# Edge stage of a graph network layer: the second layer's message stays in PSUM, and the first half of the pipeline moves by one slot

## What is computed

```python
x = concatenate((h[i], h[j], w), axis=-1)
msg = silu(x @ mW1 + mb1)
msg = layer_norm(msg, ln_g, ln_b)
msg = silu(msg @ mW2 + mb2)
agg = segment_sum(msg, i, num_segments=3125)
```

## The kernel before

| step | engine, line | slot |
|---|---|---|
| gather of 2 x 128 rows of `b_table` into `g_rows` | GpSimd, L961 | p |
| one-hot `ohT` of the target, from `loc_rows` (loaded by SyncE) | VectorE, L1164 | p+1 |
| first matmul, row of `a_sb` into `psH` | TensorE, L1057 | p+2 |
| `g_rows` += `psH` ("hid") | VectorE, L1178 | p+2 |
| silu 1 into `act1` | ScalarE, L1006 | p+4 |
| statistics (two `bn_stats`) | VectorE, L1184 | p+4 |
| variance (five small steps), each three pairs | VectorE, L1130 to L1142 | at j = 1, 4 |
| power -1/2 of the variance ("root"), each three pairs | GpSimd, L950 | at j = 0, 3 |
| shift, each three pairs | VectorE, L1150 | at j = 0, 3 |
| normalisation into `normed` (two) | ScalarE, L992 | p+10 |
| four transposes into `psM` | TensorE, L1077 | p+11 |
| copy to `nT` | ScalarE, L1002 | p+12 |
| second layer into `ps2` (four fp32 matmuls, eight passes) | TensorE, L1085 | p+13 |
| silu 2 from `ps2` to `msg` | ScalarE, L985 | p+15 |
| `high` = `msg` rounded to fp32r | ScalarE, L998 | p+15 |
| one-hot `ohf` of the target | VectorE, L1169 | p+15 |
| `low` = `msg` - `high` | VectorE, L1190 | p+15 |
| sum of high and low parts by target into `psG` | TensorE, L1067, L1068 | p+17 |
| `agg` += `psG` | VectorE, L1117 | p+18 |

## Time and profile before

### The profile page before, as it was taken

The page is one execution under the profiler, slowest core; times in us unless marked ns, Lnnn a source line. Parts: engine busy times, 40 slices in busy tenths (PEclk is TensorE's granted clock), DMA queues, the critical chain, the costliest instruction groups (busy, mean ns, idle before and its releaser), DMA issues. The chain is left out here.

```text
span 2091.9 us, 47075 instructions
## 1 busy us (share of the span) xinstructions
PE 1826.6 (87%) x11556; PEld 1598.7 (76%) x11557; DVE 1833.0 (88%) x4668; ACT 1501.9 (72%) x3084; POOL 1412.2 (68%) x1354
## 2 busy tenths in 40 slices
PE   3545664379999999999999999999999999999996
PEld 2434553268899898989989989989898999777774
DVE  5988999469999999999999999999999999554995
ACT  2322331279999999999999999999999999523321
POOL 6566887577888888888888888888888886013000
PEclk8987986589999999999999999999999999999998
DMA  4000100444333333333333333333333335101001
GB/s 135 1 3 20 30 28 19 121 139 143 102 104 102 107 100 107 101 107 102 105 104 103 102 101 106 101 106 101 107 100 106 102 106 75 44 0 31 1 1 62
DMA packets 109823, 169.20 MB, mean 81 GB/s; under 512 B 42786, under 2 KB 79572, under 8 KB 109518
## 3 DMA queue, kind: packets, MB, share of 16 engines
q0 software_dynamic: 43168, 114.55, 21.5%
q1 hardware_dynamic: 61086, 48.90, 7.6%
q10 hardware_dynamic: 5516, 5.08, 0.8%
HBM read 156.30 MB, written 11.74 MB: 80 GB/s over the span
## 5 line engine op out<-in xcount | busy, mean ns | idle before, releaser
L961 POOL DMA_INDIRECT g_rows<-b_table,idx_ring x816 | 847.2, 1038 | 238.8 <-issue 213.8
L1085 PE MATMUL ps<-w2g,nT 128*128 128x256 f32 x3432 | 813.6, 380 | 1.2 <-ACT rec L985 1.2
L1085 PEld LDWEIGHTS ps<-w2g,nT 128*128 128x128 f32 x3432 | 619.6, 191 | 68.2 <-ACT rec L985 1.5
L992 ACT ACTIVATE normed<-act,rec 128x255 f32<-128x255 f32 x858 | 467.7, 596 | 84.3 <-DVE rec L1150 81.4
L1057 PE MATMUL psH<-a_sb,ohT 128*128 x1716 | 345.7, 324 | 38.8 <-DVE ohT L1164 35.7
L1057 PEld LDWEIGHTS psH<-a_sb,ohT 128*128 128x128 f32 x1716 | 258.2, 192 | 93.6 <-issue 70.3
L1184 DVE BATCH_NORM_STATS2 rec<-act 128x6 f32<-128x256 f32 x858 | 317.2, 410 | 1.9 <-ACT act L1006 1.9
L1178 DVE TENSOR_TENSOR g_rows<-psH,g_rows 128x512 f32<-128x512 f32 x429 | 292.8, 682 | 9.7 <-DMA g_rows<-b_table,rec 7.6
L1190 DVE TENSOR_TENSOR low<-rec,high 128x512 fp32r<-128x512 f32 x429 | 291.5, 680 | 7.3 <-ACT high L998 7.3
L1006 ACT ACTIVATE act<-g_rows 128x512 f32<-128x512 f32 x429 | 267.5, 623 | 14.0 <-DVE g_rows L1178 13.8
L998 ACT ACTIVATE high<-rec 128x512 fp32r<-128x512 f32 x429 | 266.8, 622 | 0.2
(11 more groups left out here) (204 smaller groups left out, 2311.9 us busy)
## 6 DMA issues: line engine op xcount, KB each, us to landing
loc_rows<-loc_d SPq DMA_DIRECT2D x143, 187.5 KB
g_rows<-b_table,idx_ring POOLq DMA_INDIRECT x816, 2.8
h_sb<-in_x SPq DMA_DIRECT2D x1, 3125.0 KB
b_table<-b_out SPq DMA_DIRECT2D x25, 125.0 KB
x_all<-in_x ACTq DMA_DIRECT2D x1, 3125.0 KB
out<-x_all SPq DMA_DIRECT2D x5, 625.0 KB
ohT<-ew_d SPq DMA_DIRECT2D x143, 9.0 KB
idx_ring<-rec SPq DMA_DIRECT2D x136, 3.0 KB
```

Source lines behind the costliest of these rows:

```text
L961: pool.indirect_dma_start(g_rows[:, j, n, :], None, b_table[:, :], bass.IndirectOffsetOnAxis(ap=which, axis=0)).then_inc(s_gather[j], 16)
L992: ins = nc.scalar.activation(normed[:, (j - 10) % 2, n, 0:D - 1], act1[:, (j - 10) % RING, n, 0:D - 1], ACT.Identity, scale=rstd_e[:, g % ...
L1085: mm = pe.matmul(ps2[:, (j - 13) % 2, n, :], nT[:, (j - 13) % 2, n, q, :], w2g[:, q, :], start=(q == 0), stop=(q == 1))
```

## The change

Silu 2 writes its result back to where it came from, the bank of `ps2`; `msg` is gone. The high part is rounded from there, and the low part is `ps2` minus `high`. The second layer, which overwrites this bank, now waits for the low part (`s_low`), where it waited for silu 2 (`s_msg`). The wait for room in `high` goes from silu 2 to the high part.

All steps from the first matmul to the second layer get a lag one higher: first matmul and hid 3, silu 1 and statistics 5, variance at j = 2 and 5, shift at j = 1 and 4, normalisation 11, transposes 12, nT 13, second layer 14. Gathers, the power step, ohT, silu 2, high, ohf, low, sum and agg keep theirs. The order inside each engine's slot stays. The core of the diff (the same shift by one runs through the indices of the other steps):

```diff
-            msg = rec_rest[:, 0:6 * D].rearrange("p (k n d) -> p k n d", k=3, n=2)
...
                     if has(t, 15):
                         act.wait_ge(s_second, t - 14)
-                        need(act, s_sum, t - 17)
-                        nc.scalar.activation(msg[:, (j - 15) % 3, :, :], ps2[:, (j - 15) % 2, :, :], ACT.Silu).then_inc(s_msg, 1)
-                    if has(t, 10):
-                        g = (j - 10) // 3
+                        nc.scalar.activation(ps2[:, (j - 15) % 2, :, :], ps2[:, (j - 15) % 2, :, :], ACT.Silu).then_inc(s_msg, 1)
+                    if has(t, 11):
+                        g = (j - 11) // 3
                         act.wait_ge(s_rstd, 2 * d + g + 1)
-                        need(act, s_nx, t - 11)
+                        need(act, s_nx, t - 12)
...
                     if has(t, 15):
                         act.wait_ge(s_msg, t - 14)
-                        nc.scalar.activation(high[:, (j - 15) % 3, :, :], msg[:, (j - 15) % 3, :, :], ACT.Copy).then_inc(s_high, 1)
-                    if has(t, 12):
-                        act.wait_ge(s_nx, t - 11)
-                        need(act, s_second, t - 13)
-                        nc.scalar.activation(nT[:, (j - 12) % 2, :, :, :], psM[:, (j - 12) % 2, :, :, :], ACT.Copy).then_inc(s_nT, 1)
-                    if has(t, 4):
-                        act.wait_ge(s_hid, t - 3)
-                        need(act, s_norm, t - 9)
+                        need(act, s_sum, t - 17)
+                        nc.scalar.activation(high[:, (j - 15) % 3, :, :], ps2[:, (j - 15) % 2, :, :], ACT.Copy).then_inc(s_high, 1)
+                    if has(t, 13):
+                        act.wait_ge(s_nx, t - 12)
+                        need(act, s_second, t - 14)
+                        nc.scalar.activation(nT[:, (j - 13) % 2, :, :, :], psM[:, (j - 13) % 2, :, :, :], ACT.Copy).then_inc(s_nT, 1)
+                    if has(t, 5):
+                        act.wait_ge(s_hid, t - 4)
+                        need(act, s_norm, t - 10)
...
-                    if has(t, 13):
-                        pe.wait_ge(s_nT, t - 12)
-                        need(pe, s_msg, t - 14)
+                    if has(t, 14):
+                        pe.wait_ge(s_nT, t - 13)
+                        need(pe, s_low, t - 15)
...
-                    if has(t, 4):
-                        q = (j - 4) % RING
-                        dve.wait_ge(s_act1, t - 3)
+                    if has(t, 5):
+                        q = (j - 5) % RING
+                        dve.wait_ge(s_act1, t - 4)
...
-                        V.tensor_tensor(low[:, k, :, :], msg[:, k, :, :], high[:, k, :, :], ALU.subtract).then_inc(s_low, 1)
+                        V.tensor_tensor(low[:, k, :, :], ps2[:, (j - 15) % 2, :, :], high[:, k, :, :], ALU.subtract).then_inc(s_low, 1)
```

More of the change, by code:

```diff
@@ L983, in slot @@
                         act.wait_ge(s_second, t - 14)
-                        need(act, s_sum, t - 17)
-                        nc.scalar.activation(msg[:, (j - 15) % 3, :, :], ps2[:, (j - 15) % 2, :, :], ACT.Silu).then_inc(s_msg, 1)
-                    if has(t, 10):
-                        g = (j - 10) // 3
+                        nc.scalar.activation(ps2[:, (j - 15) % 2, :, :], ps2[:, (j - 15) % 2, :, :], ACT.Silu).then_inc(s_msg, 1)
+                    if has(t, 11):
+                        g = (j - 11) // 3
                         act.wait_ge(s_rstd, 2 * d + g + 1)
-                        need(act, s_nx, t - 11)
+                        need(act, s_nx, t - 12)
                         for n in range(2):
-                            k = 2 * ((j - 10) % 3) + n
-                            ins = nc.scalar.activation(normed[:, (j - 10) % 2, n, 0:D - 1], act1[:, (j - 10) % RING, n, 0:D - 1],
+                            k = 2 * ((j - 11) % 3) + n
+                            ins = nc.scalar.activation(normed[:, (j - 11) % 2, n, 0:D - 1], act1[:, (j - 11) % RING, n, 0:D - 1],
                                                        ACT.Identity, scale=rstd_e[:, g % 2, k:k + 1],
@@ L997, in slot @@
                         act.wait_ge(s_msg, t - 14)
-                        nc.scalar.activation(high[:, (j - 15) % 3, :, :], msg[:, (j - 15) % 3, :, :], ACT.Copy).then_inc(s_high, 1)
-                    if has(t, 12):
-                        act.wait_ge(s_nx, t - 11)
-                        need(act, s_second, t - 13)
-                        nc.scalar.activation(nT[:, (j - 12) % 2, :, :, :], psM[:, (j - 12) % 2, :, :, :], ACT.Copy).then_inc(s_nT, 1)
-                    if has(t, 4):
-                        act.wait_ge(s_hid, t - 3)
-                        need(act, s_norm, t - 9)
-                        nc.scalar.activation(act1[:, (j - 4) % RING, :, :], g_rows[:, (j - 4) % RING, :, :],
+                        need(act, s_sum, t - 17)
[7 more added lines that the diff above has]
+                        need(act, s_norm, t - 10)
+                        nc.scalar.activation(act1[:, (j - 5) % RING, :, :], g_rows[:, (j - 5) % RING, :, :],
                                              ACT.Silu).then_inc(s_act1, 1)
@@ L1037, in prepare @@
                 def prepare(d):
-                    lo = d * RING - 2
+                    lo = d * RING - 3
                     n0, n1 = 0, RING
@@ L1046, in slot @@
                 def slot(t, d, j):
-                    if has(t, 2):
-                        k = (j - 2) % RING
+                    if has(t, 3):
+                        k = (j - 3) % RING
                         if k % 3 == 0:
-                            pe.wait_ge(s_ew_in[k // 3], 16 * (d + 1 if j >= 2 else d))
-                        pe.wait_ge(s_ohT, t - 1)
-                        need(pe, s_hid, t - 3)
+                            pe.wait_ge(s_ew_in[k // 3], 16 * (d + 1 if j >= 3 else d))
+                        pe.wait_ge(s_ohT, t - 2)
+                        need(pe, s_hid, t - 4)
                         b = pe.snap(regs[j], min_val=0, max_val=BLOCKS - 1)
@@ L1056, in slot @@
                                 rows = a_sb[:, bass.ds(b, 1), part, :].rearrange("p a n -> p (a n)")
-                                mm = pe.matmul(psH[:, j % 2, n, :], ohT[:, k, n, :], rows,
+                                mm = pe.matmul(psH[:, (j - 3) % 2, n, :], ohT[:, k, n, :], rows,
                                                start=(part == 0), stop=(part == 1))
@@ L1069, in slot @@
                         mm.then_inc(s_sum, 1)
-                    if has(t, 11):
-                        if isinstance(t, int) and t == 11:
+                    if has(t, 12):
+                        if isinstance(t, int) and t == 12:
                             pe.wait_ge(s_one, 1)
-                        pe.wait_ge(s_norm, t - 10)
-                        need(pe, s_nT, t - 12)
+                        pe.wait_ge(s_norm, t - 11)
+                        need(pe, s_nT, t - 13)
                         for n in range(2):
                             for q in range(2):
-                                mm = pe.transpose(psM[:, (j - 11) % 2, n, q, :], normed[:, (j - 11) % 2, n, q * P:(q + 1) * P],
+                                mm = pe.transpose(psM[:, (j - 12) % 2, n, q, :], normed[:, (j - 12) % 2, n, q * P:(q + 1) * P],
                                                   identf[:, :])
                         mm.then_inc(s_nx, 1)
-                    if has(t, 13):
-                        pe.wait_ge(s_nT, t - 12)
-                        need(pe, s_msg, t - 14)
+                    if has(t, 14):
+                        pe.wait_ge(s_nT, t - 13)
+                        need(pe, s_low, t - 15)
                         for n in range(2):
                             for q in range(2):
-                                mm = pe.matmul(ps2[:, (j - 13) % 2, n, :], nT[:, (j - 13) % 2, n, q, :], w2g[:, q, :],
+                                mm = pe.matmul(ps2[:, (j - 14) % 2, n, :], nT[:, (j - 14) % 2, n, q, :], w2g[:, q, :],
                                                start=(q == 0), stop=(q == 1))
@@ L1119, in variance @@
                 def variance(t, d, j, n):
-                    if not has(t, 7) or j % 3 != 1:
+                    if not has(t, 8) or j % 3 != 2:
                         return
@@ L1145, in shifts @@
                 def shifts(t, d, j):
-                    if not has(t, 9) or j % 3:
+                    if not has(t, 10) or j % 3 != 1:
                         return
@@ L1173, in slot @@
                     shifts(t, d, j)
[L1174 to L1178, removed]
+                    if has(t, 3):
+                        k = (j - 3) % RING
+                        dve.wait_ge(s_first, t - 2)
+                        dve.wait_ge(s_gather[k], 32 * (d + 1 if j >= 3 else d))
+                        V.tensor_tensor(g_rows[:, k, :, :], psH[:, (j - 3) % 2, :, :], g_rows[:, k, :, :],
                                         ALU.add).then_inc(s_hid, 1)
-                    if has(t, 4):
```

(5 more changed lines are left out.)

## The result

The changed kernel takes 2167.89 us (median of 4 runs, 2166.12 to 2171.92) beside 2090.18 us for the kernel before; the ratio is 1.0375, 95% interval 1.0354 to 1.0395. The profiled executions differ by 2166.12 - 2094.02 = 72.1 us. Slower was forecast, 2118 us and at most 2140; the direction came out, the size did not.

What follows compares the result with a forecast made beforehand. GpSimd was taken as the bound at 3.191 us a slot; the new loop's 3.26 over 412 slots costs 28.4 us, plus 0.4 for the last ones, giving 2118 us as median, range 2076 to 2140.

Steps and rivals of the forecast that it cites:

- Who bounds the kernel before: Edge stage: GpSimd is never free, 1198 of 1200 us, at 3.191 us a slot; then VectorE, then the other two.
- The loop: Second layer, silu 2 to silu 1, statistics to low part, second layer two pairs later: 6.52 us, 3.26 a slot.
- the way from the low part to the second layer: Loop leg from VectorE's low part's end to TensorE's second layer's start: 0.05 us, upper bound 0.15.
- ScalarE's leg: Loop leg from silu 2's start to silu 1's end: 3.08 us less 0.04 and 0.02, so 3.02.
- The two legs that end and begin with the statistics: Silu 1's end to VectorE's statistics, 0.03 us; statistics' start to the low part's end, 1.33 us.
- the passes: Loop leg of the second layer's eight passes on TensorE: 1.99 us with weights not preloaded, lower bound 1.89.
- the way from them to silu 2: Loop leg from the end of TensorE's passes to ScalarE's start: 0.10 us.
- All wait in this loop, none adds to it: Engines' own slots, VectorE 3.0, ScalarE 2.95, GpSimd below 3.1 us, all under 3.26, so nothing is added.
- rival 4: Silu, high and low wait for more than one loop, for instance at variance slots: +14 to +27 us; chance 0.10.
- signs: Edge-stage waits: TensorE for the low part in nearly every slot, 0.1 to 0.2 us; ScalarE before silu 2, about 0.3.
- Port relief: Low part with one PSUM operand stops delaying gathers by 0.45 us; GpSimd's 3.19 falls about 0.15 to 0.3 per slot.
- Rival 1: Shorter loop and freed GpSimd leave TensorE at its 3.10 floor: -37 us, 2052 us; chance 0.16 with partial gains.

Runs made afterwards that it cites:

- e1: Lags of the change alone against the kernel before, silu 2 writing msg in SBUF, second layer waiting for silu 2: 2114.88 us.
- e11: e10 with the message in SBUF and the second layer waiting for silu 2 alone: 2153.68 us.
- e13: e1 with the second layer waiting for the low part, a wait no buffer needs there: 2180.2 us.
- e10: Changed kernel with VectorE's low part moved ahead of the statistics and their wait for silu 1: 2063.52 us.
- e4: Changed kernel with silu 1 moved in ScalarE's slot to behind the normalisation, before high and nT: 2083.0 us.
- e3: Changed kernel with TensorE's load of six block numbers moved from the turn's start to the last slot before it: 2132.26 us.

## Why the prediction was right or wrong

**Who bounds the kernel before: right.** GpSimd had 1198 of 1200 us, with gaps of 0.29 us a gather. In the runs with the message in SBUF and no wait for the low part (e1, e11) GpSimd again has no gap beyond that.

**The loop: right in every link.** e13 (the wait alone brings it), e10 and e4 (moving one instruction out of it breaks it) show it. Its legs summed to 6.52 us and measured 6.59. Too short were the way from the low part to the second layer, 0.14 for 0.05, where the prediction had taken the lower of two rows, and ScalarE's leg, 3.06 for 3.02, since silu 2 gained nothing from PSUM and nT and silu 1 lost 0.01 each. The two legs that end and begin with the statistics were 0.01 short each. Too long were the passes, 1.97 for 1.99, and the way from them to silu 2, 0.04 for 0.10, which partly offset it. In 412 slots 0.035 us is 14 us.

**"All wait in this loop, none adds to it": the step that failed.** The prediction compared the engines' own work with 3.26 and found all below. TensorE's 3.10 had been read from one slot of the drain, which has no turn in it, and so the load at the turn was not in the sum at all: 1.47 us in TensorE's queue behind the newly late second layer. It adds 0.09 us a slot, 36 us (e3). The prediction asked what stands behind the waiting low part and behind silu 1, and did not ask it for TensorE's own new wait. Its rival 4 had the right form, something that runs into the loop once in a few slots, but named VectorE's variance steps, at 14 to 27 us; e3, whose slot is that of the loop's legs, leaves nothing for them.

The sum then reads 28.4 + 14 + 36 = 78 us, for 78 in the medians and 72 in the profiled executions. The agreement is partly luck: by the trace's own slot the turn adds 0.076 us, 31 us and not 36, and the sum is 74.

Of its signs one came out only in part. The second layer follows the low part closely in four slots of six and not in nearly every one, and ScalarE's and VectorE's waits stand in about every second slot (178 and 187 of 356), ScalarE's with 0.53 us each where 0.3 was forecast.

**Port relief: right, and hidden.** Gathers beside the low part fell from 1.40 to 0.96 us and GpSimd's work below the slot; in the changed kernel it bought waiting time only. The relief is not whole, since `ohf` still holds gathers up (148 of 675 are over 1.1 us, up to 1.25). Rival 1, in which it decides, is what e10 turned into: 2063.5 us, for 2052 worked out.

**ohT's wait, SyncE's loads, the shift: right.** TensorE's wait for the one-hot is gone from the list, no wait for a load appears, and VectorE's wait for GpSimd fell to 1.8 us.

## What to carry to other kernels

When a buffer's release moves from one engine's instruction to another's, write down the loop that the new wait closes, with every instruction that stands in order ahead of the releasing one, and divide its length by the number of buffers; then ask again what stands behind the new wait on the waiting engine, register loads at a loop's turn too, which show in no busy time. If such a loop is too long, look for an instruction in it that only the written order puts there: here one moved low part turned +3.7% into -1.2%. And an edit that covers a stall is worth what covers it: the same early load gained 36 us under a wait and lost 40 where the wait had gone.

## What was not expected of the hardware

TensorE's load of six registers from SBUF takes 0.81 to 1.49 us of its sequencer in the kernel before (60 loads) and 1.46 to 1.49 in the changed one, VectorE's load of one about 0.3 us (304 ns in the median). GpSimd's gathers of 0.95 us and its power instruction of 1.36 us were up to 0.55 us longer beside VectorE instructions with two SBUF operands, and a moved lag changed how many of them met: 1038, 1114 and 1094 ns in the mean for the same gathers, in the kernel before, e1 and e11. ScalarE's silu from and to the same PSUM bank ran as fast as into SBUF, 582 and 587 ns.
